# Rows laid from ScalarE's queue, fewer units ahead of batch 0, and an attention and coupling order placed beat by beat

## The reference, cut to what matters

```
x = x + layernorm(attention(layernorm(x)))     # 16 heads of 8; q, k, v from the left 128 features
y = layernorm(x)
gf = global_net(mean of y over the tokens)
out = y
for _ in range(3):
    tf = sigmoid(w4 gelu(w3 gelu(w2 gelu(w1 out))))      # 256 -> 256 -> 128 -> 64 -> 1
    out = out + (0.1 + range * (0.7 gf + 0.3 tf - 0.5) * 2) * twist(out)
x = x + layernorm(out)
```

## Time and profile before

| | |
|---|---|
| median of 3 runs | 3891.49 us (3891.26 to 3892.51) |
| the profiled execution | 3891.38 us |
| its span, first to last instruction | 3889.5 us |
| time around the span | 1.9 us |
| PE busy | 91% |
| DVE busy | 81% |
| ACT busy | 76% |
| POOL busy | 23% |
| granted TensorE clock, mean | 0.95 |

### The profile page before, as it was taken

The page is one execution under the profiler, slowest core; times in us unless marked ns, Lnnn a source line. Parts: engine busy times, 40 slices in busy tenths (PEclk is TensorE's granted clock), DMA queues, the critical chain, the costliest instruction groups (busy, mean ns, idle before and its releaser), DMA issues.

```text
span 3889.5 us, 56225 instructions
## 1 busy us (share of the span) xinstructions
...
## 2 busy tenths in 40 slices
...
GB/s 65 55 2 41 27 7 61 1 77 2 45 33 1 77 2 77 2 31 47 1 77 2 76 2 18 60 2 77 2 70 8 2 76 2 66 2 33 2 22 22
DMA packets 48407, 123.70 MB, mean 32 GB/s; under 512 B 13569, under 2 KB 14977, under 8 KB 40065
## 3 DMA queue, kind: packets, MB, share of 16 engines
...
...
## 4 chain that ended last, share of the span: by engine, by line
PE 51%; ACT 23%; DVE 9%; POOL 6%; issue 6%; DMA 2%; SPq 2%; ACTq 0%; POOLq 0%; DVEq 0%
ACT p_sb L582 17%; PE heads_ps L396 16%; PE ring_ps L358 10%; PE scoresT_ps L381 9%; PE scoresT_ps L494 6%; DVE max_parts L791 4%; PE scoresT_ps L499 2%; PE ring_ps L425 2%; DVE stats L802 1%; PE scoresT_ps L502 1%; POOL rest L977 1%; DMA q_rows<-neg_rows 1%; ACT headsT L591 1%; ACT x_in L595 1%; SPq L248 1%
## 5 line engine op out<-in xcount | busy, mean ns | idle before, releaser
L791 DVE TENSOR_REDUCE max_parts<-ring_ps 128x1 f32<-128x512 f32 x3654 | 2326.8, 683 | 375.2 <-PE ring_ps L358 348.6
L582 ACT ACTIVATE p_sb<-scoresT_ps 128x1024 f32<-128x1024 f32 x2048 | 1979.2, 1023 | 228.8 <-PE scoresT_ps L381 218.1
L358 PE MATMUL ring_ps<-k_rows,q_rows 48*128 48x512 bf16 x3654 | 1225.2, 393 | 29.8 <-DVE max_parts L791 19.6
L396 PE MATMUL heads_ps<-p_sb,v_sb 128*9 128x512 f32 x8192 | 1090.1, 605 | 13.7 <-ACT p_sb L582 13.5
L381 PE MATMUL scoresT_ps<-q_rows,k_rows 51*128 51x512 bf16 x4096 | 955.5, 389 | 101.4 <-ACT p_sb L582 61.0
L358 PEld LDWEIGHTS ring_ps<-k_rows,q_rows 48*128 48x128 bf16 x3654 | 269.0, 94 | 1037.6 <-DVE max_parts L791 896.8
L948 POOL CAST max_split<-max_all 128x16 bf16<-128x16 f32 x128 | 25.3, 198 | 2224.7 <-DVE max_all L797 2224.7
L494 PE MATMUL scoresT_ps<-state,w 128*128 128x512 f32 x768 | 396.7, 642 | 25.1 <-DVE state L844 21.9
L381 PEld LDWEIGHTS scoresT_ps<-q_rows,k_rows 51*128 51x128 bf16 x4096 | 209.9, 94 | 482.6 <-ACT p_sb L582 428.4
L692 ACT ACTIVATE p_sb<-scoresT_ps,b 128x512 f32<-128x512 f32 x192 | 131.7, 686 | 242.6 <-PE scoresT_ps L494 240.5
L396 PEld LDWEIGHTS heads_ps<-p_sb,v_sb 128*9 128x9 f32 x8192 | 122.8, 88 | 440.5 <-issue 404.2
...
## 6 DMA issues: line engine op xcount, KB each, us to landing
...
out<-x_sb SPq DMA_DIRECT2D x16, 1024.0 KB, 18.5
...
q_rows<-neg_rows SPq DMA_DIRECT2D x512, 3.0 KB
...
```

Of the source, the lines that this page charges most:

```text
L358: e.matmul(ring_bank(max_taken, u + 1), q_rows[rows, slot, pair, h * BANK + qb * P:h * BANK + (qb + 1) * P], k_rows[rows, slot, pair, kh * ...
L396: m = e.matmul(heads_ps[32 * j:32 * j + DH + 1, :], v_sb[:, b % 2, kb, 4 * (group % NG) + j, 0:DH + 1], p_sb[:, n % 2, j, :], start=(kb == ...
L582: e.activation(p_sb[:, n % 2, 2 * two:2 * two + 2, :].rearrange("p h n -> p (h n)"), scoresT_ps[:, 2 * two * BANK:(2 * two + 2) * BANK], A ...
L791: e.tensor_reduce(max_parts[:, gi % 2, kh, col:col + 1], bank_of(max_taken, u + 1), AX.X, ALU.max).then_inc(max_taken, 1)
```

## The change

- **Rows from ACT.** `lay_rows` moves from SP's list to ACT's, from beat 18 to beat 22, with all its 24 DMAs. Its wait for `pv_done` goes. SP keeps the maxima, the loads and the store.
- **Casts on ACT.** `split_mid` moves from DVE to ACT, four 128x512 casts a batch.
- **Batch 0.** Only `LEAD0 = 52` units stand ahead of its attention, all of them in the beats of b = -1 from beat 5 on. Its 64 steps carry four units each (256), its 30 beats 52, so that after them 360 units are done, as before.
- **Steps.** In the other batches the three units of a step stand as two behind the first pair of scores and one behind the weighting, none behind the second pair. 192 units stand in the steps and 64 in the beats, by a table of 30 numbers.
- **Beats.** Layer 2 of the first half comes ahead of layer 1 of the second half; the first product with the state is one beat earlier, the second one beat later; norm 0 is cut in four pieces; v is projected in beats 19 and 20; the store by POOL (`ADD_OUT`) moves from beat 17 to 19, the load of `x_sb` from ahead of the steps to beat 0. `layer 2` waits for the later of its two inputs.

```diff
-LAYERS = ((1, 0, 0), (1, 0, 1), (1, 1, 0), (2, 0, 0), (3, 0, 0), ...
+LAYERS = ((1, 0, 0), (1, 0, 1), (2, 0, 0), (1, 1, 0), (3, 0, 0), ...
-BEAT_UNITS = (3, 2, 2, 3, 3, 2, 2, 2, 2, 1)
-IN_COUPLING = 3 * sum(BEAT_UNITS)
+BEAT_UNITS = (3, 2, 2, 1, 3, 2, 2, 2, 2, 1,
+              2, 2, 2, 3, 3, 2, 2, 4, 2, 1,
+              2, 1, 2, 3, 4, 2, 2, 2, 2, 1)
+IN_COUPLING = sum(BEAT_UNITS)
...
+LEAD0 = 52
...
-LAY_ROWS = 18
-TWIST0, UPDATE0, TWIST1, UPDATE1 = 7, 8, 10, 11
+PROJECT_QK, SPLIT, PROJECT_V, LAY_ROWS = (13, 14, 15, 16), (14, 15, 16, 19), (19, 20), 22
+TWIST0, UPDATE0, TWIST1, UPDATE1 = 6, 8, 11, 11
...
         def units_in_step(b, n, third):
-            return units_by(b, min(IN_ATTENTION, 3 * n + third + 1))
+            if b < 0:
+                return 0
+            if b == 0:
+                return units_until(LEAD0 + 4 * n + (1, 3, 4)[third])
+            return units_until(b * UNITS + LEAD + min(IN_ATTENTION, 3 * n + (2, 2, 3)[third]))
 
         def units_in_beat(b, j):
-            return units_by(b, IN_ATTENTION + sum(BEAT_UNITS) * (j // CYCLE) + sum(BEAT_UNITS[:j % CYCLE + 1]))
+            if b == -1:
+                return LEAD0 * max(0, j - 4) // (BEATS - 5)
+            if b == 0:
+                return LEAD0 + 4 * STEPS + (UNITS + LEAD - LEAD0 - 4 * STEPS) * (j + 1) // BEATS
+            return units_until(b * UNITS + LEAD + IN_ATTENTION + sum(BEAT_UNITS[:j + 1])) if b > 0 else 0
...
# scalar_program, in place of sync_program
+            def lay_rows(b):
+                slot = b % 2
+                e.wait_ge(low_done, 4 * (b + 1))
...
+                        e.dma_start(rows[at:at + DH, slot, :, :],
+                                    parts[64 * side:64 * side + 64, i, term[i], :]).then_inc(laid, 16)
...
# scalar_program, in place of vector_program's tensor_copy
+            def split_mid(b, i, h):
+                e.wait_ge(rest_done, 4 * b + 2 * i + h + 1)
+                e.activation(parts[:, i, 1, h * BANK:(h + 1) * BANK], rest_sb[h], ACT.Copy).then_inc(mid_done, 1)
```

More of the change, by code:

```diff
@@ L496, in coupling @@
                 if layer == 2:
-                    e.wait_ge(hid_done, end_of(b, cycle, 1, c, 1))
+                    e.wait_ge(hid_done, max(end_of(b, cycle, 1, c, m) for m in range(2)))
                     for k in range(2):
@@ L808, in row_moments @@
                 if b:
-                    e.wait_ge(norm_act[i], (2 if i == 0 else 4) * b)
+                    e.wait_ge(norm_act[i], 4 * b)
                 for t in range(NT):
```

235 lines of the change are left out of this document (117 added, 118 removed).

## The result

| | before | after |
|---|---|---|
| median (range) | 3891.92 us (3891.26 to 3892.51) | 4162.91 us (4161.01 to 4166.7) |
| span of the profiled execution | 3889.5 us | 4159.8 us |
| granted TensorE clock, mean | 0.950 | 0.913 |

The change makes the kernel 7% slower: ratio 1.0698, 95% interval 1.0679 to 1.0716. Predicted were 4016 us with a range from 3860 to 4160, so the time is 3 us beyond its upper end. The sign was right, the size was not: +271 us instead of +125.

A forecast was written before the change was run, and what follows sets the result against it. PE, ACT and DVE were taken as near the bound in attention, PE busiest; coupling alternates PE and ACT. Terms -16 - 1.5 + 11 - 10.8 - 90 - 28 + 260 = +125 us gave 4016 us, range 3860 to 4160.

The forecast's parts named there:

- ACT is held by its issues: Coupling stages: 24 row issues stop ACT for 21.4 us; +20 us a batch, 260 us for 13 (208 to 312).
- the first rival: Row issues: ACT is not held by them, so the gains remain; -173 us, time 3718 us, chance 0.12.
- The coupling stage without its issues: Coupling stages apart from row issues: new beats save 2 us each, -28 us over 14 (0 to -56).
- The sooner product: Coupling stage: first product one beat sooner, counted with fewer PE units as -2 us a stage.
- The casts: Coupling beats 14 to 19: four casts move from DVE into ACT's gaps; no effect by themselves.
- The steps: Attentions 1 to 15: weighting starts sooner without a unit ahead; -6 us each, -90 us in all (-30 to -120).
- Start: Before attention 0: fewer units ahead, first exponential near 126 us; -16 us (-5 to -25).
- Attention 0: First attention: the wait for maxima goes, but DVE's four units a step take 159 us; -1.5 us (-5 to +3).
- Beats of b = 0: Coupling beats behind the first attention: row issues hold ACT, fewer units and casts help; +11 us (+5 to +16).
- attention 1: Second attention: its 10.83 us wait for `neg_rows` goes, -10.8 us, besides -6 us from the steps.
- Tail: Behind attention 15, with no units or rows: counted at nothing, 3 us either way.
- the third rival: Whole kernel: ACT held, new steps win nothing, PE's clock stays low; +315 us, time 4206 us, chance 0.10.

The follow-up runs named there:

- b_layers: Kernel before with single row issues on ACT in attention steps, new unit order, new start, new layer order and shifted state products: 3815.18 us, ratio 0.9801.
- act_spread: Changed kernel with the 24 row issues still on ACT, but one in every second of the next attention's first 48 steps: 3841.82 us, ratio 0.9867.
- rows_sp: Changed kernel with only the 24 row issues put back in SP's list, still at beat 22: 3885.60 us, ratio 0.9986.
- act_block: Changed kernel with all 24 row issues on ACT in one piece behind step 40 of the next attention: 4287.19 us, ratio 1.1012.
- rows_half: Changed kernel with the 12 k_rows issues in SP's list and the 12 q_rows issues in ACT's, at beat 22: 3983.75 us, ratio 1.0231.

## Why the prediction missed, step by step

- **ACT is held by its issues: right**, and the first rival (3718 us) is out. Its size was low. A block is 23.2 us in the mean, not 21.4: ACT's last three issues take 4.0, 1.55 and 1.52 us, where the last three of SP's steady block had 0.61 each. Behind the block 18.2 us passed (1107.98 to 1126.17). My 15.5 us for the work were right (18.2 less 3.1), my 1.5 us for the clock were half of the 3.1 measured. PE had its 6.4 us of work as predicted. Issues cost 287 us in all against 260, +27. Ends of 208 to 312 held it.
- **The coupling stage without its issues: the step that failed.** I put it at -28 us (0 to -56), from PE's idle time and the product that comes a beat sooner. It is +25 us over the 14 (+2.6 in each of the twelve, less in the first and last). The sooner product with the new order of layers is a gain of 0.6 us, as b_layers shows. The casts I had costed at nothing since "ACT has gaps there": but a cast waits for POOL in ACT's list, +1.1 us a stage. Units (+1.4) and v (+0.9) I had not costed place by place at all, and my ends left out a loss without a reason for it. This is +53 us of the miss.
- **The steps: the size of the term.** -90 us predicted, of them -84 for attentions 2 to 15, -39.4 measured: +45 us. The chain of the earlier trace rows was read rightly, 4.18 became 3.97 us in the pairs that nothing else holds. I multiplied it by 32 pairs; but it holds for 18 of 31, 8 win next to nothing (beside a `headsT` ACT is full), and 5 lose as much (the shown one at a join). I had seen that "some pairs are held", and took 1.4 us off for it instead of counting them.
- **Start: -8.6 instead of -16.** The block for batch 1 came where predicted (92.2 us, 23.9 long), and the maxima were negated at 116.17. What I had too short is the landing of four small DMAs that SP issues right behind. Timelines of ACT, SP and PE:

```profile
116.17 0.27 ACT L576 ACTIVATE neg_rows<-heads_ps 48x128 bf16<-48x128 f32 x1 [23.91 <-issue]
```

```profile
116.47 3.07 SPq L253 DMA_DIRECT2D q_rows<-neg_rows  x4
```

```profile
132.72 0.61 PE L383 MATMUL scoresT_ps<-q_rows,k_rows 51*128 51x512 bf16 x2 [11.24 <-DMA q_rows<-neg_rows]
```

  From the last issue's end to the scores 13.2 us pass, in which the DMA engines are 82% busy; that the rows of batch 1, still in transfer, slow the small ones is my reading and was not tested alone. Without the block (act_spread) the first exponential is at 102.9 us.
- **Attention 0 +6.0 instead of -1.5**: DVE bounds it and is busy 160.4 us, 1 us above my 159, but it is also idle for the other 5.1 of 165.5 us, which I had put at nothing; among its rows are five waits of 0.58 us and one of 1.26 for PE's matmuls. **Beats of b = 0 +13.6** for +11 and **attention 1 -16.0** for -16.8 are near by luck. Against rows_sp the issues cost these beats 15.0 us, not 18, and the fewer units and casts gave 1.4, not 7; the wait for maxima in attention 1 was worth 13.9 us, not 10.8, and the steps 2.1, not 6. **Tail +2.3**, within the 3 us allowed.
- Together 27 + 53 + 45 + 7 + 8 + 3 + 1 + 2 = 146 us, the whole of 4163 - 4016 but for 1. All of the errors point one way, half of these eight are gains counted too high (stage, steps, start, attention 0): the third rival (4206 us, "new steps win nothing", at 0.10) was nearer to the time than the forecast. Its mechanism was not: the attentions 2 to 15 won 39 us, the clock was back before the stage's end (0.96 from 1119 to 1126.2 us), and its 312 us equal the measured growth of the stages by chance, since that is 287 us of issues and 25 of beats and casts.

## What to carry to other kernels

Moving DMA issues to another engine doesn't make them cheaper, it puts them into that engine's list: place them one or two at a time behind instructions long enough to cover them, and no block where others wait for that engine's next result. When a block is priced, count its cover and the slower clock behind it separately; here they hid each other. A gain read from one pair of steps is multiplied only by the pairs that look like it; sort the steps by what bounds them first. What merely changes place needs a price per place, with a loss among the ends.

The fastest kernel here, b_layers, is the kernel before with three of the change's ideas (order of a step's units, the start, order of the layers) and its single issues on ACT: 3815.18 us, ratio 0.9801.

## What the chip showed besides

ACT's sequencer issues a 128 KB row DMA in 0.62 us, 0.03 apart, but 24 in a row take 20.5 to 24.2 us in after and act_block, as some wait. Mostly it is the last three: 5.2, 1.8 and 1.75 us in most blocks of act_block, 4.0, 1.55 and 1.52 in a steady one of after, whose third to fifth take 1.4 to 1.5 too. In SP's steady block before it is the third to eighth that take up to 1.9 us, and the last three do not wait. Twelve on ACT beside twelve on SP (rows_half) take 9.1 to 10.1 us in the steady stages, but 12.9 in one earlier, with 3.5 and 2.5 us for the last two. What an issue waits for stays open.

Behind 1.02 us exponentials ACT's sequencer starts a piece 1.47 us ahead of the next exponential in its list, and within that time issues cost nothing. A piece's price is its length less this, and more when PE's clock falls in the pause: four pieces of six cost 18.4 us where their length is 15.6.
